# Perceiver block on one core: last group's order, shift parts on GpSimd, one shift row copied by VectorE, finer waits in group 0

## What is computed

```python
q = (layernorm(x) @ Wq + bq) ; k = ctx @ Wk + bk ; v = ctx @ Wv + bv      # per head: 256x16, 4096x16
attn = softmax(clip(q @ k.T * 16**-0.5, -10000, 10000))
x = x + (attn @ v) @ Wo + bo
x = x + self_attention(layernorm(x))                                      # causal, 256 tokens
x = x + ffn(layernorm(x))                                                 # slots, top-8 routing
```

## Time and profile before

| what | value |
|---|---|
| timed runs | 1121.88, 1127.3, 1132.46 us, median 1127.3 |
| profiled execution, its own time | 1128.7 us |
| span in its profile | 1126.9 us (mean granted TensorE clock 0.976) |
| TensorE matmul busy | 1037.6 us, 92% of the span |
| VectorE, ScalarE, GpSimd busy | 826.1, 718.4, 378.5 us (73%, 64%, 34%) |
| chain that ended last | TensorE 73%, VectorE 16%, ScalarE 5% |
| from the first unit of group 0 to the last values | about 118.6 to 942.5 us |

### The profile page before, as it was taken

The page is one execution under the profiler, slowest core; times in us unless marked ns, Lnnn a source line. Parts: engine busy times, 40 slices in busy tenths (PEclk is TensorE's granted clock), DMA queues, the critical chain, the costliest instruction groups (busy, mean ns, idle before and its releaser), DMA issues.

```text
span 1126.9 us, 29329 instructions
## 1 busy us (share of the span) xinstructions
PE 1037.6 (92%) x11489; PEld 710.5 (63%) x11489; DVE 826.1 (73%) x1520; ACT 718.4 (64%) x1413; POOL 378.5 (34%) x437
## 2 busy tenths in 40 slices
PE   7799789989999899999999999999999888978997
PEld 6677566666666676766667666655655455646655
DVE  7667778878787788888888888888888123692553
ACT  2222568878787778888888887777677554414342
POOL 5633534544544454445535442040000001103320
PEclk9999899999999999999999999999999699998999
DMA  7854765555556465655547464234541100000001
GB/s 219 239 167 106 219 180 160 166 153 155 160 146 188 133 176 149 184 152 165 168 137 202 142 178 133 71 96 125 154 114 35 48 2 1 1 1 2 3 1 38
DMA packets 120724, 137.24 MB, mean 122 GB/s; under 512 B 21351, under 2 KB 92906, under 8 KB 120554
## 3 DMA queue, kind: packets, MB, share of 16 engines
q1 hardware_dynamic: 115082, 128.86, 39.8%
q10 hardware_dynamic: 5472, 6.23, 2.1%
HBM read 97.20 MB, written 37.81 MB: 120 GB/s over the span
## 4 chain that ended last, share of the span: by engine, by line
PE 73%; DVE 16%; ACT 5%; issue 4%; DMA 1%; SPq 1%; ACTq 0%; POOLq 0%; DVEq 0%
PE acc L1826 21%; PE st L1794 12%; PE mx L1780 11%; PE kps L1740 8%; DVE mxp L1218 7%; PE misc L1780 5%; DVE free_k L1473 2%; ACT prob L1026 2%; PE st L1635 1%; PE mx L1776 1%; PE setB L2082 1%; ACT prob L1113 1%; PE st L1996 1%; PE mx L1630 1%; DVE spad L1240 1%
## 5 line engine op out<-in xcount | busy, mean ns | idle before, releaser
L1218 DVE TENSOR_REDUCE mxp<-mx 128x1 f32<-128x512 f32 x709 | 464.3, 682 | 95.6 <-PE mx L1780 67.5
L1026 ACT ACTIVATE prob<-st 128x512 f32<-128x512 f32 x704 | 377.7, 597 | 130.6 <-PE st L1794 129.8
L1794 PE MATMUL st<-qst,kst 51*128 51x256 f32 x2048 | 393.1, 297 | 16.5 <-DVE flagf L1250 8.1
L1794 PEld LDWEIGHTS st<-qst,kst 51*128 51x128 f32 x2048 | 308.8, 189 | 39.6 <-ACT prob L1026 12.7
L1780 PE MATMUL mx<-kst,qst 51*128 51x512 f32 x633 | 272.7, 455 | 9.5 <-DVE mxp L1218 6.6
L1218 DVE TENSOR_REDUCE mxp<-misc 128x1 f32<-128x512 f32 x315 | 214.8, 682 | 40.0 <-PE misc L1780 39.9
L1026 ACT ACTIVATE xn<-st 128x512 f32<-128x512 f32 x320 | 172.1, 597 | 50.8 <-PE st L1794 50.5
L1826 PE MATMUL acc<-prob,v_raw 128*17 128x256 f32 x2816 | 189.6, 387 | 4.8 <-ACT prob L1026 2.7
L1780 PEld LDWEIGHTS mx<-kst,qst 51*128 51x128 f32 x633 | 116.3, 186 | 87.4 <-issue 54.2
L1780 PE MATMUL misc<-kst,qst 51*128 51x512 f32 x315 | 143.0, 454 | 9.7 <-DMA kst<-kscr 4.8
L1740 PE MATMUL kps<-w_hi,ctx_p 64*128 64x256 f32 x564 | 138.0, 307 | 0.0
(11 more groups left out here) (427 smaller groups left out, 1272.0 us busy)
## 6 DMA issues: line engine op xcount, KB each, us to landing
kst<-kscr SPq DMA_DIRECT2D x240, 128.0 KB, 2.6
kscr<-kraw SPq DMA_DIRECT2D x100, 256.0 KB, 2.6
kst<-kscr SPq DMA_DIRECT2D x240, 64.0 KB, 2.6
ctx<-in_ctxT SPq DMA_DIRECT2D x93, 128.0 KB, 2.6
ctx<-in_ctxT SPq DMA_DIRECT2D x184, 64.0 KB, 2.3
low<-lscr SPq DMA_DIRECT2D x16, 512.0 KB
kscr<-prob SPq DMA_DIRECT2D x16, 256.0 KB, 4.0
kscr<-o_sb SPq DMA_DIRECT2D x12, 256.0 KB, 2.8
```

Of the source, the lines that this page charges most:

```text
L1026: act.activation(exps(unit_at(n)), st_bank("scores", unit_at(n))[:, :], ACT.Exp).then_inc(exp_done, 1)
L1218: dve.reduce_max(at, bank_of_max(n)[:, :], AX.X).then_inc(max_red, 1)
L1794: mm = pe.matmul(st_bank("scores", n)[:, h * T:(h + 1) * T], kst[row, j // 2, at:at + P], qst[row, 2 * (q % 3) + j // 2, :], start=True, s ...
```

## The change

1. **Weights.** The order of the three splits becomes key weights, the raw second halves of both, value weights. VectorE makes two `w_lo` ahead of the units and the third behind its second maximum of group 0. The projections wait for the `w_lo` at the product that reads it, and only for as many as it needs.
2. **SyncE's queue at the start of group 0.** The two loads of `bo` go from ahead of the loop to the fifth eighth of group 0; `read_low(0)` goes behind the first block load and the ctx load of the first eighth.
3. **Shift parts.** The four small operations leave VectorE. GpSimd makes the parts in five (`shift_parts`, with a new tile `sneg`), between `k_split` and `ctx_split` of the seventh eighth of each group, and for group 0 ahead of the `k_split` of piece 16. `turn_shift` waits for `m_clip` too.
4. **Shift rows.** ScalarE copies the rows 32 to 34 alone; VectorE copies 96 to 98, behind the flag's maximum of unit 60.
5. **Last group.** TensorE's order in group 15 becomes: two units, values, two units (the second is the first of the next step), `finish` and `slot_products`.

```diff
@@ weights, SyncE @@
-        weights = (key weights, value weights, (w_raw, w_hi[:, :, 1, :], w_lo[:, :, 1, :]))
+        weights = (key weights, (w_raw, w_hi[:, :, 1, :], w_lo[:, :, 1, :]), value weights)
-            for n, name in enumerate(("L0_xattn_bo", "L0_attn_bo")):
-                sp.dma_start(bo[:, n, :], ...)
             write_low(0)
-            read_low(0)
...
+                    if q == 0 and k == 0:
+                        read_low(0)
+                    if q == 0 and k == 4:
+                        for n, name in enumerate(("L0_xattn_bo", "L0_attn_bo")):
+                            sp.dma_start(bo[:, n, :], ...)
@@ GpSimd @@
+            def shift_parts(q):
+                if q == NQ:
+                    return
+                pool.wait_ge(m_clip, 2 * q + 1)
+                wait(pool, shift_ps, q)
+                pool.tensor_scalar(sparts[:, :, :, 0], shift[:, :, :], -1.0, None, ALU.mult).then_inc(m_1, 1)
+                pool.tensor_scalar(sneg[:, :, :], shift[:, :, :], -1.0, None, ALU.mult).then_inc(m_res, 1)
+                pool.wait_ge(m_1, q + 1)
+                pool.wait_ge(m_res, 2 * q + 1)
+                pool.tensor_tensor(sres[:, :, :], sneg[:, :, :], sparts[:, :, :, 0], ALU.subtract).then_inc(m_res, 1)
+                pool.wait_ge(m_res, 2 * q + 2)
+                pool.tensor_copy(sparts[:, :, :, 1], sres[:, :, :]).then_inc(m_2, 1)
+                pool.wait_ge(m_2, q + 1)
+                pool.tensor_tensor(sparts[:, :, :, 2], sres[:, :, :], sparts[:, :, :, 1], ALU.subtract).then_inc(m_3, 1)
...
                     for k in range(8):
                         if k % 2 == 0 and k_job(q, k) is not None:
                             k_split(k_job(q, k))
+                        if k == 6:
+                            shift_parts(q + 1)
                         ctx_split(q, k + 2)
@@ ScalarE, VectorE @@
-                for r in (32, 96):
-                    act.activation(qst[r:r + 3, at:at + 2, :], shift_bank(q)[r:r + 3, :]...)
+                act.activation(qst[32:35, at:at + 2, :], shift_bank(q)[32:35, :]...)
...
                     dve.tensor_reduce(flagf[0:1, :], shift_bank(q)[0:1, 0:P], AX.X, ALU.max,
                                       apply_absolute_value=True).then_inc(flag_abs, 1)
+                    dve.tensor_copy(qst[96:99, 2 * (q % 3):2 * (q % 3) + 2, :], shift_bank(q)[96:99, :]...)
@@ TensorE @@
-                        wait(pe, weights_set, 0 if split_at[q, k] else 4)
+                    if split_at[q, k] < 2 and g == 0 and part == 0 and w is w_lo:
+                        pe.wait_ge(weights_set, 4 if m else 2 if n == 0 else 3)
...
+                if q == NQ - 1:
+                    if t % 4:
+                        continue
+                    for u in (n + 1, n, n + 2) if t == 0 else (n, n + 2):
+                        score_half(u, 0)
+                        score_half(u, 1)
+                    values((n - 4) // UQ, (n - 4) % UQ // 4)
+                    for u in (n + 3, n + 5) if t < UQ - 4 else (n + 3,):
+                        score_half(u, 0)
+                        score_half(u, 1)
+                    if t == 4:
+                        finish(q - 1)
+                    for at in range(t, t + 4):
+                        slot_products(at)
+                    continue
```

More of the change, by code:

```diff
@@ L121, in build @@
         sres = sb("sres", [P, 4, QT])
+        sneg = sb("sneg", [P, 4, QT])
         spad = sb("spad", [P, QT, 4, 64], BF16)
@@ L455, in move_block @@
                               src[:, 0:1, :].rearrange("(i e d) r t -> e (d r) i t", i=2, e=2)[e]).then_inc(done, 16)
-        weights = ((wk[:, 0, :], w_hi[:, 0, 0, :], w_lo[:, 0, 0, :]), (wv[:, 0, :], w_hi[:, 1, 0, :], w_lo[:, 1, 0, :]),
-                   (w_raw, w_hi[:, :, 1, :], w_lo[:, :, 1, :]))
+        weights = ((wk[:, 0, :], w_hi[:, 0, 0, :], w_lo[:, 0, 0, :]), (w_raw, w_hi[:, :, 1, :], w_lo[:, :, 1, :]),
+                   (wv[:, 0, :], w_hi[:, 1, 0, :], w_lo[:, 1, 0, :]))
         @block.sync
@@ L730, in _ @@
                 pool.wait_ge(part_step, n + 1)
+            pool.wait_ge(rows_set, 4)
+            shift_parts(0)
             def ctx_split(q, k):
@@ L1232, in shift_step @@
                                       apply_absolute_value=True).then_inc(m_clip, 1)
-                    dve.tensor_scalar(sparts[:, :, :, 0], shift[:, :, :], -1.0, None, ALU.mult).then_inc(m_1, 1)
-                elif t == 54:
-                    dve.wait_ge(m_1, q + 1)
-                    dve.scalar_tensor_tensor(sres[:, :, :], shift[:, :, :], -1.0, sparts[:, :, :, 0],
-                                             ALU.mult, ALU.subtract).then_inc(m_res, 1)
-                elif t == 55:
-                    dve.wait_ge(m_res, q + 1)
-                    dve.scalar_tensor_tensor(sparts[:, :, :, 1], sres[:, :, :], 1.0, sres[:, :, :],
-                                             ALU.mult, ALU.max).then_inc(m_2, 1)
-                elif t == 56:
-                    dve.wait_ge(m_2, q + 1)
-                    dve.wait_ge(m_clip, 2 * q + 2)
-                    dve.tensor_tensor(sparts[:, :, :, 2], sres[:, :, :], sparts[:, :, :, 1],
-                                      ALU.subtract).then_inc(m_3, 1)
                 elif t == 60:
@@ L1251, in shift_step @@
                                       apply_absolute_value=True).then_inc(flag_abs, 1)
+                    dve.tensor_copy(qst[96:99, 2 * (q % 3):2 * (q % 3) + 2, :], shift_bank(q)[96:99, :].rearrange(
+                        "p (i t) -> p i t", i=2)).then_inc(shift_set, 1)
                 elif t == 61:
@@ L1337, in _ @@
             dve.wait_ge(k_ps, KLEAD)
-            for raw, hi, lo in weights:
+            for raw, hi, lo in weights[0:2]:
                 dve.tensor_tensor(lo, raw, hi.bitcast(F32), ALU.subtract).then_inc(weights_set, 1)
@@ L1382, in _ @@
                     reduce_unit(n + AHEAD)
+                if n == 1:
+                    raw, hi, lo = weights[2]
+                    dve.tensor_tensor(lo, raw, hi.bitcast(F32), ALU.subtract).then_inc(weights_set, 1)
                 if t == 7 and q > 0:
@@ L1801, in turn_shift @@
                 pe.wait_ge(m_3, q + 1)
+                pe.wait_ge(m_clip, 2 * q + 2)
                 if q:
@@ L1970, in _ @@
                     finish(q - 1)
-                if q == NQ - 1 and t % 4 == 3:
-                    for at in range(t - 3, t + 1):
-                        slot_products(at)
             values(NQ - 1, 15)
```

9 lines of the change are left out of this document (6 added, 3 removed).

## The result

The changed kernel takes 1141.07 us (median of 20 runs, 1128.84 to 1170.12), the kernel before 1126.96 us beside it (20 runs, 1120.44 to 1133.49). The ratio is 1.0089, 95% interval 1.0066 to 1.0112. The prediction was 1112 us in a range of 1103 to 1121; the kernel became slower, not faster. The ratio leaves out executions that a long stretch of half clock draws out, the median doesn't, which is why the two differ.

What follows compares the result with a forecast made beforehand. The prediction took TensorE to be the bound, losing time where its steps aren't even. Its terms, -9.9 + 8.4 - 6.5 - 7.7 - 0.35 = -16 us from 1128.7, gave 1112.7 (1111.3 against the median); it said 1112, range 1103 to 1121.

Steps and rivals of the forecast that it cites:

- Two of its own signs of being wrong: Wrong if new waits for GpSimd stand at TensorE, or if the last group's steps stay above 3.2 us.
- Parts off VectorE, -9.9: Step making the shift parts, groups 0 to 10: 1.05 us shorter, less 0.15 of waiting; 0.90 x 11 = -9.9 us.
- Queued behind the parts is ctx_split ..., so the delay goes no further.: GpSimd's queue behind the parts: ctx_split is read two steps later, the next waits for TensorE's projection anyhow; no cost.
- The copy, +0.6 at 14 boundaries: Group boundaries: VectorE's copy queues behind the flag, so the bank is free 0.6 us later; +8.4 us over 14.
- Start of group 0, -6.5: Start of group 0: key block 12 is issued 5.6 us sooner and waits for `w_lo` are finer; -6.5 us.
- Last group, -7.7: Group 15: two units ahead of the slots keep ScalarE in work; slot steps 2.9 us instead of 3.46; -7.7 us.
- The rival that the last group leaves the half clock earlier: Last group stays at full clock as the wait before it shrinks; 6 to 8 us more gain, 1105 us; chance 0.13.
- Last boundary, -0.35: Last group boundary: no maximum ahead of the flag, TensorE waits 0.85 us for ScalarE and gains 0.35.
- The slower rival: At `turn_shift`: the parts' chain on GpSimd bounds every boundary, each us beyond 1.17 costing 11 us; 1142 at 4 us; chance 0.05.

Runs made afterwards that it cites:

- combined: The kernel before with parts 1, 2 and 3, GpSimd's once-only work of group 12 ahead of its shift parts; 1112.52 us, ratio 0.9904.
- combined_late: combined with GpSimd's once-only work of group 12 back behind the shift parts; 1123.36 us, ratio 0.9951.
- copy_busy: combined_copy with the product of the second max unit behind the shift computed five times into the same bank; 1119.26 us, ratio 0.9926.
- combined_copy: combined with part 4 added, VectorE's copy behind the flag; 1130.00 us, ratio 1.0040.
- start_only: The kernel before with parts 1 and 2 alone; 1117.95 us, ratio 0.9924.
- scalar_rows: The changed kernel with both shift rows copied by ScalarE again, part 4 undone; 1135.72 us, ratio 1.0009.
- copy_only: The kernel before with part 4 alone; 1148.87 us, ratio 1.0118.
- third_copy: combined with a third ScalarE copy of a shift row, into a spare tile, ahead of the two real ones; 1122.52 us, ratio 0.9955.
- last_only: The kernel before with part 5 alone; three of 4 runs at 1160.58 to 1163.29 us, one at 1124.04.
- copy_early: The changed kernel with VectorE's flag maximum and copy ahead of the maximum of unit 60's turn, groups 1 to 15; 1137.64 us, ratio 0.9997.

## Why the prediction was wrong

Built up part by part, the kernels stand at -12.5 us against their runs of before (combined), +5.0 (with the copy), +5.8 (with part 5 too) and +14.1 (the change, whose constants come late); by the ratios -10.8, +4.5, +5.1 and +10.0. So three steps of the prediction failed: the copy's wait was priced by its length alone, the queue behind the parts at nothing, and the last group as a gain. Two of its own signs of being wrong came true, new waits for GpSimd at TensorE and slot steps over 3.2 us.

- **Parts off VectorE, -9.9.** Right in mechanism and nearly in size. The step of the parts loses 1.11 us in 11 groups, the next one grows by 0.30, since the turn waits for the last part: 0.81 us, 8.9 in all. The five operations take 0.26, 0.23, 0.21, 0.22 and 0.23 us, 1.39 from first start to last end, against the 1.25 of the sum, and so the turn is 0.31 us late and not 0.15.
- **"Queued behind the parts is ctx_split ..., so the delay goes no further."** This step failed. I looked at what is queued behind the parts in a middle group, not at what GpSimd's program has behind them in every group. In group 12 it is 13 us of once-only work, and it made the last step 2.9 us longer in the changed kernel, with half clock from the handover in it, and 4.8 to 7.2 us in the five others that have it. Price 7.6 us: combined_late is 4.9 us under its runs of before, combined 12.5 us (5.3 by the ratios). At equal half clock 2.8 us of it are left.
- **The copy, +0.6 at 14 boundaries.** It measured +0.67 in 11 of them and +0.65 in the three others. The mechanism, queued behind the flag, was right, and slightly undersized since the copy doesn't overlap its neighbours: it starts 0.03 us behind the flag's end, while the flag starts 0.08 us before the end of the maximum ahead of it. The Trainium skill (VectorE: DVE Perf Modes, Two Vector instructions with no wait between them) holds an instruction until earlier ones have finished where it starts in another quadrant of partitions, and the copy starts at partition 96 between two that start at 0; the trace agrees, though no run here moved it. What failed is that a wait was priced as its length only. A longer idle time of TensorE can also bring half clock, and copy_busy prices that at 14.0 us (9.0 us under its runs of before, where combined_copy is 5.0 over; 12.8 by the ratios).
- **Start of group 0, -6.5.** Right in mechanism, and the size lies within what was measured: -8.6 us (-11.9 to -5.2 by the interval of start_only), -4.3 at equal half clock. In its profile the first six steps together are 5.0 us shorter. That the first scores came 3.9 us later in the changed kernel's profile, at 122.56 against 118.65, is no cost of parts 1 to 3: combined, which has them, has its first scores at 118.76.
- **Last group, -7.7.** This step failed: nothing was gained. I took 0.2 us for a unit that isn't held up; a pair takes 0.67 from start to start, 0.33 each, and the values 0.99 instead of 0.88. TensorE's own work in a slot step is then 3.33 us, not the 2.8 to 2.9 of the sum, and against 3.46 only 0.13 is won; steps without slots stay at 2.61. At half clock the three first steps are 7.88, 6.14 and 8.01 us instead of 7.63, 5.65 and 4.67. The rival that the last group leaves the half clock earlier did not come with part 5: the profiles with it show 20.5 to 99 us of half clock there, before's 20.5. It was nearer the mark for part 4: with the copy and before's order the profiles show 3.4 us (combined_copy), twice 3.4 (copy_only) and 10.2 (copy_busy). But one without the copy, combined, has 3.4 as well, so this is not shown.
- **Last boundary, -0.35.** The handover of group 14 takes 3.01 us instead of 3.62, and TensorE's wait there is 0.66 instead of 0.85: -0.6.
- **The slower rival** looked for the parts' own chain on GpSimd. The queue behind it was the mechanism, and neither that nor the clock was among the cases, so 0.06 for slower and the upper end of 1121 us were too small.

## What to carry to other kernels

An instruction with a wait that is put into an in-order queue delays everything behind it, once-only work of one iteration included: list the whole queue behind the new wait for every iteration, not for a typical one. Price an idle time of a nearly full TensorE with the half clock that may follow it, and look at the spread of the timed runs and at their granted clock before reading medians. A reordering that leaves TensorE without a pause is no gain when it was the next bound anyhow; work out its own time per step, from start to start, before counting the waits as gain.

## What was unexpected of the hardware

- An idle time of 1.0 to 1.2 us in an otherwise full TensorE was followed by a stretch of 3.4 us or more at 1.2 GHz in some groups and not in others of the same execution, 21 of 70 in the counts above; one of 0.6 us or less never was, at 168 handovers. What decides it within an execution stays open.
- Half clock can last while TensorE is busy 10.00 us of 10: 68 us in group 13 of scalar_rows, 72 us in copy_only and third_copy, and some 70 of the 99 us in and behind the last group of last_only and copy_early. In groups 0 to 10, where projections are in the steps, the stretches seen behind a handover or a group's end were 3.4 us. Why it lasts in the one place and not in the other stays open; no run here tells it apart.
- From the end of GpSimd's last instruction to the values that its reading of the flag lets go it was 3.0 to 5.4 us at the end of group 12 in the six profiles with late constants (791.68 to 794.72 in the changed kernel). Work at the end of a group is late that much earlier than it looks.
